# Selective scan: softplus factors, delta*u and output product one state later, and TensorE's sum ahead of the convolution in state 2

## The reference

```python
u = silu(conv(x_in) + conv_b)
x_dbl = u @ xproj_w.T                       # dt (8), B (16), C (16)
delta = softplus(dt @ dt_w.T + dt_b)
dA  = exp(delta * A[:, n])                  # for each of 16 states n
dBu = delta * u * B[n]
h = dA * h + dBu                            # along the 512 tokens
y = sum_n h[n] * C[n] + u * Dp
out = (y * silu(z)) @ out_w.T
```

## Time and profile before

| | |
|---|---|
| median of 3 runs | 4125.07 us (4122.55 to 4131.44) |
| profiled execution, its own time | 4125.14 us |
| its span in the trace | 4123.3 us |
| busy in the span | PE 81%, VectorE 62%, ScalarE 45%, GpSimd 29% |
| first and last scan of the block start at | 2302.8 and 3262.2 us |

### The profile page before, as it was taken

How to read it: one execution, slowest core, us unless ns; L and a number is a source line. 1 busy time by engine, 2 the same in 40 slices (tenths; PEclk the granted TensorE clock), 3 DMA queues, 4 the chain that set the end, 5 groups by cost and what they waited for, 6 DMA issues and landing times. The chain is left out here.

```text
span 4123.3 us, 47666 instructions
## 1 busy us (share of the span) xinstructions
PE 3348.2 (81%) x12605; PEld 1558.2 (38%) x12605; DVE 2546.5 (62%) x3960; ACT 1843.5 (45%) x2855; POOL 1192.4 (29%) x1006
## 2 busy tenths in 40 slices
PE   5599986999996499877798688788788768569998
PEld 2122225444443255433444233333333344434443
DVE  6788864333346477645433799988998753554444
ACT  2166652444435255534233677667677413202222
POOL 3211110000002222200000699889889600100000
PEclk7699996999997699979799899989989969769999
DMA  4522110000004632110000333334333110000000
GB/s 137 130 60 60 59 45 0 0 0 0 0 26 116 157 100 86 52 31 0 0 0 22 124 144 144 133 137 149 127 142 144 72 39 0 2 0 0 0 0 20
DMA packets 131062, 253.69 MB, mean 62 GB/s; under 512 B 24773, under 2 KB 100954, under 8 KB 113434
## 3 DMA queue, kind: packets, MB, share of 16 engines
q1 hardware_dynamic: 126842, 250.55, 18.9%
q0 software_dynamic: 4096, 1.59, 0.2%
HBM read 191.98 MB, written 56.89 MB: 60 GB/s over the span
## 5 line engine op out<-in xcount | busy, mean ns | idle before, releaser
L941 DVE TENSOR_REDUCE a_top<-a_sc 128x1 f32<-128x512 f32 (+3 forms) x1024 | 544.7, 584 | 167.4 <-PE a_sc L818 95.1
L1917 POOL TENSOR_TENSOR a_g<-a_g,a_spread 128x1024 f32<-128x1024 f32 x256 | 599.6, 2361 | 46.7 <-DVE a_g L1861 46.5
L1861 DVE TENSOR_TENSOR_SCAN a_g<-a_decay,a_drive 128x512 f32<-128x512 f32 x512 | 588.3, 1201 | 7.0 <-ACT a_drive L1777 6.7
L899 ACT ACTIVATE a_prob<-a_st 128x1024 f32<-128x1024 f32 (+2 forms) x512 | 419.1, 862 | 321.8 <-PE a_st L835 205.1
L455 DVE TENSOR_TENSOR f_s<-f_a,f_spread 128x512 f32<-128x512 f32 x392 | 268.0, 687 | 433.8 <-ACT f_a L440 267.1
L1633 PE MATMUL a_y<-a_g,ident 128*128 128x512 f32 x1024 | 490.6, 620 | 49.3 <-POOL a_g L1917 46.2
L422 PE MATMUL f_y<-f_s,f_w 128*128 128x512 f32 x784 | 400.9, 598 | 21.4 <-DVE f_s L455 20.8
L415 PE MATMUL f_hid<-h,f_w 128*128 x784 | 403.7, 600 | 6.1 <-PEq L246 6.1
L815 PE MATMUL a_sc<-a_k,a_q 96*128 96x512 bf16 (+3 forms) x1024 | 308.0, 356 | 41.9 <-DMA a_k<-a_k_rows 39.4
L1756 ACT ACTIVATE a_decay<-a_delta,a_capped_a 128x512 f32<-128x512 f32 x512 | 331.8, 710 | 9.3 <-DVE a_g L1861 8.7
L1633 PEld LDWEIGHTS a_y<-a_g,ident 128*128 128x128 f32 x1024 | 201.0, 200 | 333.0 <-issue 242.8
(11 more groups left out here) (334 smaller groups left out, 4933.7 us busy)
## 6 DMA issues: line engine op xcount, KB each, us to landing
a_spread<-a_bc_rows SPq DMA_DIRECT2D x128, 1024.0 KB, 4.7
a_q<-a_q_rows SPq DMA_DIRECT2D x64, 288.0 KB
a_pv_rows<-a_pv_sb SPq DMA_DIRECT2D x64, 256.0 KB, 2.1
a_q_rows<-p_qp SPq DMA_DIRECT2D x72, 128.0 KB
a_q_rows<-a1q_qp SPq DMA_DIRECT2D x72, 128.0 KB
a_k_rows<-a1q_kp SPq DMA_DIRECT2D x72, 128.0 KB
a_k<-a_k_rows SPq DMA_DIRECT2D x32, 288.0 KB
a_k_rows<-p_kp SPq DMA_DIRECT2D x72, 64.0 KB
```

Source lines behind the costliest of these rows:

```text
L899: nc.scalar.activation(prob[w % 2][:, j, 0:width(kp)], st[:, j % 2, 0:width(kp)], ACT.Exp, scale=a.scale).then_inc(s.exp_done, 1)
L941: nc.vector.tensor_reduce(top[:, t, n:n + 1], sc[:, slot(4 * n + t) % 3, 0:w], AX.X, ALU.max).then_inc(s.maxed, 1)
L1861: nc.vector.tensor_tensor_scan(g[:, n % 8, k, way], decay[:, n % 4, k, way], drive[:, k, way], 0.0, ALU.mult, ALU.add).then_inc(scanned, 1)
L1917: nc.gpsimd.tensor_tensor(g[:, n % 8, :, :], g[:, n % 8, :, :], spread[:, pair % 4, 2 + n % 2:3 + n % 2, :].to_broadcast([P, H2, L]), ALU. ...
```

## The change

In `pe_unit` the sum of y over a finished state goes ahead of the convolution's halves in states 2 and 3; the output product moves from state 13 to 14, and the convolution for the unit after the next from states 14 and 15 (a half each) to state 15 (whole). In `dve_unit` the four factors move from states 9 to 12 to states 10 to 13, delta behind them. In `pool_unit` delta * u moves from before state 13 to before state 14. `act_unit` and `sp_unit` are not in the diff.

```diff
@@ pe_unit
                     if n == 0 and d == 1 and projects:
                         pe_project(b - 1, U - 2)
+                    if n >= LAG:
+                        pe_gate_sum(U, d, n - LAG)
+                    elif not first:
+                        pe_gate_sum(U - 1, 1 - d, STATES - LAG + n)
                     if n in (2, 3) and not last_unit:
                         if n == 2:
                             nc.tensor.wait_ge(soft_read, 2 * U + 1)
                             wait(nc.tensor, o_done, U - 1)
                             wait(nc.tensor, p_done, b - 1 if d == 0 else b)
                         pe_conv(nb, nd, 0, (3, 2) if n == 2 else (1, 0))
-                    if n >= LAG:
-                        pe_gate_sum(U, d, n - LAG)
-                    elif not first:
-                        pe_gate_sum(U - 1, 1 - d, STATES - LAG + n)
                     if not last_unit:
                         if n == 4:
                             pe_z(nb, nd, U + 1)
...
-                    if n == 13 and not first:
+                    if n == 14 and not first:
                         if not last_unit:
                             nc.tensor.wait_ge(dve_step, STEPS_DVE * (U + 1) + 1)
                         pe_out(b if d == 1 else b - 1, U - 1, 1 - d)
-                    if n in (14, 15) and ahead:
-                        if n == 14:
-                            nc.tensor.wait_ge(dve_step, STEPS_DVE * (U + 1) + 1)
-                        pe_conv(b + 1, d, 1, (3, 2) if n == 14 else (1, 0))
+                    if n == 15 and ahead:
+                        nc.tensor.wait_ge(dve_step, STEPS_DVE * (U + 1) + 1)
+                        pe_conv(b + 1, d, 1)
@@ dve_unit
-                    if 9 <= n < 9 + len(LOG1P):
-                        dve_factor(nd, U + 1, n - 9)
-                    if n == 8 + len(LOG1P):
+                    if 10 <= n < 10 + len(LOG1P):
+                        dve_factor(nd, U + 1, n - 10)
+                    if n == 9 + len(LOG1P):
                         dve_delta(nd, U + 1)
@@ pool_unit
-                    if n == STATES - 3 and not last_unit:
+                    if n == STATES - 2 and not last_unit:
                         pool_du(U + 1, 1 - d)
```

## The result

| | before | after |
|---|---|---|
| median of executions | 4128.25 us (4 runs, 4122.55 to 4139.27) | 4189.61 us (4 runs, 4181.03 to 4198.31) |
| ratio, 95% interval | | 1.0145 (1.0111 to 1.018) |
| profiled execution: time, span | 4125.14, 4123.3 us | 4182.97, 4181.2 us |

The changed kernel is slower by 61 us in the medians and by 57.8 in the profiled executions. (The medians of before differ by a few us from one comparison to the next, since more executions joined; each ratio stands against those of its own comparison.) From the first scan to the last gating the block took 970.5 us (2302.8 to 3273.3) and takes 1025.8 (2303.3 to 3329.1): 55.3 us, nearly all of it.

A forecast was written before the change was run, and what follows sets the result against it. VectorE was taken to set the pace. Copy waits less the earlier scans +78.0, gating stops -15.6 and z at full clock -8.4 gave +54 us on the profiled 4125.14: 4179 us, range 4164 to 4199.

The forecast's parts named there:

- Step 1: VectorE's stop before the first softplus factor goes; state 10's scans start 3.36 us earlier, real gain 2.24 a unit.
- F0: VectorE's first of four softplus factors; the stop before it, 3.68 us in an even unit, was to go.
- S10: VectorE's pair of scans of state 10 (S13: of state 13), to start 3.36 us earlier in the even unit.
- Steps 2 and 3: Scans of states 11 and 13 wait for ScalarE copies queued behind squares: 3.11 and 4.33 us lost per unit.
- Delta*u: GpSimd's product and ScalarE's copy of it, one state later: cost nothing; without cover up to 3.4 us a unit.
- rival (e): TensorE's sum moved ahead does nothing, y hanging on something other than its queue: +16 us, 4195; chance 0.08.
- rival (a): TensorE's z products stay slow: 4187 us; chance 0.22.
- rival (d): TensorE's low clock lasts beyond the output product after 10 us idle: up to 4246 us, half 4212; chance 0.06.
- z's term: TensorE's z products at full clock bring decay 10 1.20 us earlier in seven even units: -8.4 us.
- Rival (c): Only the loss before state 13's scans bites, state 11's copy being early: +7 us, 4132; chance 0.04.
- Rival (b): Copies of drive 11 and 13 reach the scans in time, so their losses vanish: 4076 us; chance 0.05.
- the gating's gain: VectorE's 13 stops before the gating, waiting for TensorE's sum of y, shrink by 1.2 us each: -15.6 us.

The follow-up runs named there:

- Experiments 1 to 3: The changed kernel with ScalarE's copies of drive 11 and 13 one square earlier: both 4075.58 us, copy 11 alone 4137.98, copy 13 alone 4119.47.
- Experiments 4 and 5: The changed kernel with TensorE's sum put back behind the convolution, 4211.45 us; the kernel before with only that sum moved ahead, 4101.57 us.
- experiment 1: The changed kernel with ScalarE's copies of drive 11 and 13 both one square earlier: 4075.58 us, ratio 0.9875.
- Experiment 8: The kernel of experiment 1 with the row maximum of delta kept in PSUM in place of SBUF: 4063.2 us, ratio 0.9841.

## Why the prediction was right

The prediction was 4179 us, range 4164 to 4199; measured 4189.61 in the median, 4182.97 in the profiled execution, on which the sum was made. Point by point:

- **Step 1, the stop before F0 goes, S10 waits for decay 10.** Predicted a wait of 0.6 to 1.5 us for decay 10. Measured 0.50 to 0.57 in 12 units and 1.22 to 1.35 in 3. The last three are units in which TensorE's product for delta (L1682) runs in part at the low clock, 3.05 to 3.09 us for four passes against 1.98 (granted clock 0.62 in the one shown), which was not foreseen:

```profile
2712.53 3.08 PE L1682 MATMUL a_bank<-a_xp,a_dt_w 8*128 8x512 f32 x4 [1.40 <-ACT a_xp L1732]
```
- **Steps 2 and 3, the copies.** Predicted stops of 3.1 and 4.3 us, 15 each, some 110 in all; measured 3.03 and 4.25, 113.3 with the short ones. The sums of four and five terms, read from starts in the timeline before, were right to 0.1 us. Experiments 1 to 3 show the cause, since each stop goes with its copy alone.
- **Delta*u.** Predicted free. The only wait for it is one of ScalarE, 7.1 us at the block's start, and the kernel before has the same. No run moved delta*u or the output product alone: that these parts of the change cost nothing rests on the list of waits.
- **TensorE.** The gating's stops were to lose 15.6 us and lost 14.2; the odd units with a projection stop 1.25 to 1.91 (1.26 predicted), even ones not at all (0.1 predicted). Experiments 4 and 5 put this part and the clock of z together at 25.7 and 25.6 us of the block, and so rival (e), that the sum ahead does nothing, falls.
- **The clock.** z took 1.98 us in all 15 units, so rival (a) falls; rival (d), the low clock lasting longer after 10 us of idle, does too: 3.78 us for the four output passes (granted clock 0.50), then 1.88 in the sum behind (1.00). By the Trainium skill's two levels (TensorE: Matmul & The Clock Gate, Part 1) the longer idle was to cost nothing at its start; the trace agrees, 3.78 after 10.21 us as after 5.88. The reason given for z, that 1.80 us of idle had left four passes at 1.98, is no rule, though: in experiment 1's kernel the output product takes 3.68 us after 2.00 us of idle in one unit (granted clock 0.52) and 1.98 after 2.02 in another (1.00). And z's term was sized too large, 8.4 us: in experiments 4 and 5 the stops that hang on it, before S10 and before F0, changed by 5.7 and 4.7.
- **The sum.** +54 predicted; +55.3 in the scan block. Some of this closeness is luck, for small errors cancel: the two long stops were 2.4 us smaller than predicted (109.2 for 111.6), the short ones for copies 2.6 smaller, which stood in no term, while F0's stops less the wait of S10 gave back 38.5 in place of 42.0 (33.6 and the 8.4 of z), TensorE gave 1.4 less, and the overlap lost at stops is 1.4. None of them touches the mechanism.
- **Outside the block.** The profiled spans differ by 57.9, so 2.6 us lie outside the block, 0.4 ahead of it and 2.1 behind; and the medians differ by 61, with the executions of the changed kernel spread over 17 us. No edit touches the parts of the program that run ahead of this one, and yet its first scan starts anywhere from 2298.9 to 2310.1 us in the eleven profiled executions. What moves it was not settled; for the same reason the block is the better measure of a single edit here.

Rival (c), only the stop of S13, falls with the 15 stops of 3.03. Rival (b), faster, was priced at 4076 by supposing the copies on time. That is what experiment 1 made true by an edit: 4075.58. Its price left out z's gain (8.4 by the prediction's own term) and the port wait described below (19.1 us more in that kernel), and put the gating's gain at 15.6 where it was 23.2; these pull in opposite ways, so the closeness is in part luck.

## What to carry to other kernels

When a step moves in one engine's hand-written list, look at every other engine that hands it something in order: a step that waits for the moved one takes all that stands behind it along, here a copy that had nothing to do with the factor. The two stops here could be priced before the run from starts in one timeline, each to 0.1 us, by writing out the queue of the engine that is waited for. A change that loses may be one edit short: ask what would have to move with it.

## What the runs showed of the hardware that was not expected

A VectorE operation on 128x2 elements takes 0.17 us when GpSimd is idle, and up to 2.39 when it is not. In experiment 1's kernel, VectorE and then GpSimd:

```profile
2691.95 1.66 DVE L1833 TENSOR_SCALAR a_peak<-a_peak 128x2 f32<-128x2 f32 x1
```

```profile
2688.91 4.68 POOL L1916 TENSOR_TENSOR a_g<-a_g,a_spread 128x1024 f32<-128x1024 f32 x2
2694.55 2.35 POOL L1902 TENSOR_TENSOR a_du_s<-a_delta,a_u 128x1024 f32<-128x1024 f32 x1 [0.96 <-DVE a_capped_a L1836]
```

The small operation ends at 2693.61, within 0.02 us of GpSimd's two products (2688.91 + 4.68 = 2693.59). It is so in all 15 units: the end lies 0.02 to 0.03 us behind that of the product that GpSimd has in hand. Such a wait stands in no list of waits: it is inside the duration. The reduction before it, with its result in SBUF too, isn't lengthened (1.22 us). The Trainium skill (SBUF — State Buffer, Who interferes with whom) says that VectorE and GpSimd share a pair of SBUF ports that one instruction locks whole, and that `tensor_scalar` between SBUF operands can want it while `tensor_reduce` never does. Experiment 8 agrees: with the operand in PSUM the duration is 0.17 us in all 16 calls, and in 14 of them GpSimd is at work. In the kernels before and after it was 0.17 as well, and there GpSimd stands idle at each of the 16 calls; with both copies on time VectorE comes to the operation sooner, while GpSimd still works, and that brought the wait out.
